# Graph attention's first fetch: attention columns as the weights, logits kept as rows in DRAM

## The reference

```
xl = (x @ W_l).reshape(n, H, C);  xr = (x @ W_r).reshape(n, H, C)
feat = xl[src] + xr[dst]
feat = jnp.where(feat >= 0, feat, NEG_SLOPE * feat)
logits = jnp.einsum('ehc,hc->eh', feat, att)
seg_max = jax.ops.segment_max(logits, dst, num_segments=n)
ex = jnp.exp(logits - seg_max[dst])
```

## Time and profile before

| | before |
|---|---|
| median of 3 runs, us | 10185.92 |
| profiled execution, us | 10172.71 |
| its span, us | 10170.6 |
| mean granted clock of TensorE, share of 2.4 GHz | 0.751 |
| PE / DVE / ACT / POOL busy, us | 5979.7 / 4870.8 / 2036.9 / 6515.4 |
| first fetch, 255 to 1640 us | 1385 |

### The profile page before, as it was taken

The page is one execution under the profiler, slowest core; times in us unless marked ns, Lnnn a source line. Parts: engine busy times, 40 slices in busy tenths (PEclk is TensorE's granted clock), DMA queues, the critical chain, the costliest instruction groups (busy, mean ns, idle before and its releaser), DMA issues. The chain is left out here.

```text
span 10170.6 us, 136884 instructions
## 1 busy us (share of the span) xinstructions
PE 5979.7 (59%) x24639; PEld 4757.3 (47%) x24640; DVE 4870.8 (48%) x14032; ACT 2036.9 (20%) x5514; POOL 6515.4 (64%) x9285
## 2 busy tenths in 40 slices
PE   4788885774666666645555344555455465455544
PEld 2677774553544444433334233444344344444443
DVE  6455556776644444445556333334333342455555
ACT  2111111783322222210000100001000031223324
POOL 3777772000058888888888688884888816777750
PEclk9788887997877777766667677777777765667767
DMA  4555555663067777764444333332333325677764
GB/s 151 169 173 178 171 176 195 200 199 108 2 105 105 105 105 104 105 112 135 140 139 130 120 89 90 88 90 80 89 89 89 90 83 158 223 231 241 249 201 158
DMA packets 863543, 1389.54 MB, mean 137 GB/s; under 512 B 114551, under 2 KB 516805, under 8 KB 862997
## 3 DMA queue, kind: packets, MB, share of 16 engines
q0 software_dynamic: 315328, 634.04, 27.7%
q1 hardware_dynamic: 366180, 501.57, 15.2%
q10 hardware_dynamic: 181488, 248.03, 7.3%
HBM read 955.84 MB, written 427.35 MB: 136 GB/s over the span
## 5 line engine op out<-in xcount | busy, mean ns | idle before, releaser
L1030 POOL DMA_INDIRECT regionB<-table,gather_rows x3136 | 3105.2, 990 | 1007.2 <-POOLq L1032 606.5
L1771 POOL DMA_INDIRECT scatter_sums<-regionC,idx x880 | 1388.3, 1578 | 306.2 <-issue 246.6
L1136 PE MATMUL ps_p<-regionB,hot 128*128 x3520 | 1039.8, 458 | 768.3 <-DVE regionC L1197 576.8
L1136 PEld LDWEIGHTS ps_p<-regionB,hot 128*128 128x128 f32 x3520 | 815.6, 235 | 977.1 <-issue 833.9
L1033 POOL MEMSET regionA<- 128x192 f32 x3920 | 1124.8, 287 | 5.8 <-remote 1.6
L1136 PE MATMUL ps_p<-regionC,hot 128*128 x1760 | 646.2, 511 | 554.4 <-issue 433.3
L1030 POOL DMA_INDIRECT regionC<-table,gather_rows x784 | 755.2, 963 | 156.6 <-issue 99.3
L2113 PE MATMUL ps_p<-regionA 128*128 128x264 f32 x1760 | 578.4, 497 | 417.9 <-PEq L2108 191.7
L1136 PEld LDWEIGHTS ps_p<-regionC,hot 128*128 128x128 f32 x1760 | 440.4, 257 | 760.1 <-issue 691.4
L1844 PE MATMUL psC<-regionC 128*128 128x128 f32 x1760 | 371.2, 377 | 647.0 <-PEq L1842 644.6
L1203 DVE TENSOR_TENSOR regionA<-ps_own,own_bias 128x256 f32<-128x256 f32 x98 | 41.6, 425 | 1371.0 <-DVEq L1202 1014.9
(11 more groups left out here) (366 smaller groups left out, 10280.1 us busy)
## 6 DMA issues: line engine op xcount, KB each, us to landing
regionA<-edge_rows SPq DMA_DIRECT2D x440, 256.0 KB, 3.3
regionA<-edge_rows ACTq DMA_DIRECT2D x440, 256.0 KB
edge_rows<-regionB SPq DMA_DIRECT2D x196, 512.0 KB
edge_rows<-regionB SPq DMA_DIRECT2D x392, 256.0 KB
regionC<-srcrow_d SPq DMA_DIRECT2D x220, 256.0 KB
scatter_sums<-zero_rows ACTq DMA_DIRECT2D x8, 6400.0 KB, 41.5
regionB<-table,gather_rows POOLq DMA_INDIRECT x3136
regionA<-scatter_sums ACTq DMA_DIRECT2D x49, 1024.0 KB
```

The source lines that it names most:

```text
L1030: g.indirect_dma_start(out=rows_of(b * per + j), out_offset=None, in_=table, in_offset=bass.IndirectOffsetOnAxis(ap=idx[:, column:column + ...
L1136: x = te.matmul(ps[(u.c * VG + j) % NB], hot[:, b, 2 * j + k, :], at_tile(G, slot[j] * 2 + k), start=k == 0, stop=k == 1)
L1771: g.indirect_dma_start(out=scat, out_offset=bass.IndirectOffsetOnAxis(ap=idx[:, b, j:j + 1], axis=0), in_=sums[:, b, j, :], in_offset=None ...
```

## The change

The roles in `logit` are exchanged: the attention columns (128x4) are the weights, and the transposed features of both steps of a visit (256 columns) are streamed against them, in two halves of the feature dimension. The result stands by head on 4 partitions. Two visits fill a PSUM bank; then ScalarE copies the 4x512 rows into SBUF and writes them by DMA to a new DRAM table `logits_by_step` of 880 x 4 x 128 (`logits_out`, now in ScalarE's list with a lag of 11). VectorE no longer copies logits, and the zeroing of `LG` goes. In the softmax SP loads that table, step on partitions, in seven transfers; the 28 transposes and seven masked copies become four multiplications in place. Before the last transfer, VectorE zeroes the last block of the target, and SP waits for that.

```diff
@@ -714,18 +715,24 @@
                                 if by_step:
                                     load(sp, valid, step_d.rearrange('p (c e) -> p c e', e=P))
                                     load(sp, etcol, et_d, allow_slow_non_contiguous=True)
+                                    for c in range(SB - 1):
+                                        load(sp, RS[:, :, c, :], logits_d[c * P:(c + 1) * P, :, :])
+                                    sp.wait_ge(aux_free[0], 1)
+                                    sp.sem_inc(aux_free[0], -1)
+                                    load(sp, RS[0:S - (SB - 1) * P, :, SB - 1, :], logits_d[(SB - 1) * P:S, :, :])
                                 loaded(sp)
                                 sp.sem_inc(aux_full[0], 1)
...
+                            if by_step:
+                                v.memset(RS[:, :, SB - 1, :], 0.0).then_inc(aux_free[0], 1)
...
-                                for c in range(SB):
-                                    b = c % 2
-                                    v.wait_ge(res_full[b], 1)
-                                    v.sem_inc(res_full[b], -1)
-                                    v.tensor_tensor(RS[:, :, c, :], ps[b][:, 0:512].rearrange('p (h e) -> p h e', e=P), valid[:, c, :].unsqueeze(1).to_broadcast([P, H, P]), ALU.mult).then_inc(own_v, 1)
-                                    v.wait_ge(own_v, 1)
-                                    v.sem_inc(own_v, -1)
-                                    v.sem_inc(res_free[b], 1)
+                                for h in range(H):
+                                    v.tensor_tensor(RS[:, h], RS[:, h], valid, ALU.mult)
...
-                        for t_ in turns(a, NV, 2 * VG, 9, written_out=True):
...
+                        def logits_out(u):
+                            q = u.val // 2
+                            b = q % 2
+                            if u.val % 2 == 0:
+                                return
+                            a.wait_ge(aux_full[b], 1)
+                            a.sem_inc(aux_full[b], -1)
+                            if q >= 2:
+                                a.wait_ge(s_load[b].sem, q // 2 * 16 + s_load[b].base)
+                            a.activation(rows_out[:, b, :], psL[b][0:HEADS0, :], ACT.Copy).then_inc(own_a, 1)
+                            a.wait_ge(own_a, 1)
+                            a.sem_inc(own_a, -1)
+                            a.sem_inc(aux_free[b], 1)
+                            a.dma_start(logits_d[4 * q:4 * q + 4, :, :].rearrange('s h e -> h s e'), rows_out[:, b, :].rearrange('h (s e) -> h s e', e=P)).then_inc(s_load[b].sem, 16)
+                        for b in (0, 1):
+                            a.sem_inc(aux_free[b], 1)
+                        for t_ in turns(a, NV, 2 * VG, 11, written_out=True):
...
+                            if t_.has(11):
+                                logits_out(t_.at(11))
+                        for b in (0, 1):
+                            a.wait_ge(aux_free[b], 1)
+                            a.sem_inc(aux_free[b], -1)
+                            a.wait_ge(s_load[b].sem, NV // 4 * 16 + s_load[b].base)
...
                         def logit(u):
-                            b, gb = (u.c % 2, u.c // VG % 2)
+                            b, gb = (u.c % 2, u.c // 2 % 2)
                             te.wait_ge(act_full[b], 1)
                             te.sem_inc(act_full[b], -1)
-                            if u.c % VG == 0:
+                            if u.c % 2 == 0:
                                 te.wait_ge(aux_free[gb], 1)
                                 te.sem_inc(aux_free[gb], -1)
-                            for k in (0, 1):
-                                col = (u.c % VG * 2 + k) * HEADS0
-                                for c in (0, 1):
-                                    x = te.matmul(psL[gb][:, col:col + HEADS0], featT[:, b, 2 * k + c, :], attc[:, c, :], start=c == 0, stop=c == 1)
-                            if u.c % VG == VG - 1:
+                            both = featT[:, b].rearrange('p (k c) n -> p c k n', c=2)
+                            for c in (0, 1):
+                                x = te.matmul(psL[gb][0:HEADS0, b * 2 * P:(b + 1) * 2 * P].rearrange('h (k n) -> h k n', k=2), attc[:, c, :], both[:, c], start=c == 0, stop=c == 1)
+                            if u.c % 2:
                                 x.then_inc(aux_full[gb], 1)
...
-                        v.memset(LG[:, :, :], 0.0).then_inc(own_v, 1)
-                        v.wait_ge(own_v, 1)
-                        v.sem_inc(own_v, -1)
-                        for b in (0, 1):
-                            v.sem_inc(aux_free[b], 1)
...
-                        def logits_out(u):
-                            gb = u.c // VG % 2
-                            if u.c % VG != VG - 1:
-                                return
-                            v.wait_ge(aux_full[gb], 1)
-                            v.sem_inc(aux_full[gb], -1)
-                            v.tensor_copy(LG[:, bass.ds((u.val - (VG - 1)) * 2, GS), :], psL[gb][:, 0:GS * HEADS0].rearrange('p (s h) -> p s h', h=HEADS0)).then_inc(aux_free[gb], 1)
-                        for t_ in turns(v, NV, 2 * VG, 7, written_out=True):
+                        for t_ in turns(v, NV, 2 * VG, 3, written_out=True):
```

More of the change, by code:

```diff
@@ L140, in build @@
         wgt_d = dram('weights_by_step', [P, S])
+        logits_d = dram('logits_by_step', [S, HEADS0, P])
         srccol_d = dram('sources_by_step', [P, S])
@@ L721, in _ @@
                         def _(te):
-                            for c in range(SB):
-                                b = c % 2
[L724 to L728, removed]
+                            if not by_step:
+                                for c in range(SB):
+                                    b = c % 2
+                                    te.wait_ge(res_free[b], 1)
+                                    te.sem_inc(res_free[b], -1)
+                                    for h in range(H):
+                                        x = te.transpose(ps[b][:, h * P:(h + 1) * P], mine[:, c * P:(c + 1) * P, h], ident[:, :])
+                                    x.then_inc(res_full[b], 1)
                             if by_step:
@@ L1259, in attention_fetch0 @@
             spread = part(room, RG0 * EG * D + GS * P, [2, GS * P])
+            rows_out = part(room, RG0 * EG * D + 3 * GS * P, [2, 4 * P])[0:HEADS0]
             s_rows = plain_rows
@@ L1434, in attention_fetch0 @@
             s_used.base += NV
+            for b in (0, 1):
+                s_load[b].base += 16 * (NV // 4)
             for b in range(RG0):
```

4 lines of the change are left out of this document (removed).

## The result

The changed kernel took 10123.8 us (median of 5 runs, 10104.6 to 10144.0), the kernel before 10183.4 us on the same chip (10169.6 to 10193.1): a ratio of 0.9943, 95% interval 0.9926 to 0.996. That is 60 us faster. The forecast of 10065 us lies 118 us under the kernel before; the direction and the wide range (9955 to 10210) held, the size and the forecast's own range (10025 to 10115) did not.

The account below looks back on a forecast made before the run. TensorE sets the fetch's pace while its clock is low, POOL's gathers would at high clock. Fetch -133, stage end +4, softmax +14 make -115 us against 10172.7, giving 10058; with the runs' higher median, 10065 was said, range 9955 to 10210.

Parts of the forecast that it names:

- The clock: First fetch, TensorE: clock returns within about one visit after a stall; a third of 471 us remains, saving 153 us.
- The first rival: First fetch, TensorE after a stall: four-column logits do not lift the clock; about 10215 us, chance 0.20.
- the price of a visit at full clock: First fetch, TensorE: 0.05 us more on each of 400 visits at 2.4 GHz, costing 20 us; visit 2.19 us.
- The third rival: First fetch: stalls spread as faster TensorE leaves POOL fewer pauses; half the saving given back, about 10140 us, chance 0.13.
- eight instructions fewer a visit: First fetch: argument against spreading stalls, that eight of 32 instructions go from each visit.
- The logits on TensorE: First fetch: four 256-column records at the fetch's price, +0.05 us a visit at 2.4 GHz, +0.15 at 1.2 GHz.
- my bound of +0.15: First fetch, TensorE logits: upper bound on the direct cost per visit in us; the lower bound was -0.41.
- POOL as the bound: First fetch: rival that POOL's gathers bound throughout; its 173 us of waiting included, 193 us go, about 10010 us, chance 0.17.
- The seam: Start of softmax: logit loads +17 us, multiplications replacing masked copies -3, together +14 us.
- my upper bound: Start of softmax: +30 us, if loads in 512-byte pieces run at half speed.
- The end of the stage: End of first fetch: waits for a DMA instead of a VectorE copy of 0.18 us, +4 us.
- ScalarE and VectorE in the fetch: First fetch: VectorE's dropped logit copies (20 us) worth nothing; ScalarE's added 205 us of copies and DMA issues cost nothing.

Follow-up runs that it names:

- e9: The kernel before, unaltered, traced on chip 8; its fetch ended at 1630.1 us.
- e10: The changed kernel, unaltered, traced on chip 8; its fetch ended at 1573.9 us.
- e13: Changed kernel with attention columns zero-padded to 128 and zero rows held behind the logits' loads, chip 3; 0.9932 of the kernel before.
- e14: Changed kernel with attention columns zero-padded to 128, chip 3, all gathers; its fetch ended at 1580.5 us.
- e15: Same kernel as e14, run again on chip 3 for the spread between executions; its fetch ended at 1576.4 us.
- e2: Kernel before with each fetch matmul issued twice (1760 more 256-column records), chip 15; 10055.9 us, 1.0078 of the kernel before.
- e16: Changed kernel with columns padded to 128 and every second node-row gather of the first fetch left out, chip 3; fetch ended at 1240.0 us.
- e12: Changed kernel (4 columns) with every second node-row gather of the first fetch left out, chip 8; fetch ended at 1336.8 us.
- e7: Changed kernel with columns padded to 128 and POOL's memset behind each gather of this fetch 288 columns instead of 192; fetch ended at 1529.8 us.
- e8: As e7, but with a memset of 64 columns; 1.0112 of the kernel before, fetch ended at 1646.5 us.
- e4: Changed kernel with ScalarE's zero rows held until SP's softmax loads landed, chip 15; first VectorE work 11.7 us after first load, not 22.9.
- e1: Changed kernel with attention columns zero-padded to 128, chip 15; 0.9959 of the kernel before, fetch ended at 1512.3 us.

## Why the prediction was right, and where it failed

*The clock: right in its sum, in part by luck.* A third of the 471 us at 1.2 GHz should remain, 157; measured are 2 x (1 - 0.95) x 1319 = 132. But the reason given was a clock that comes back within about one visit of a stall. It comes back after 7.5 us in the mean, three visits, against 11.1 before; the rest comes of falls that went from 42 to 18 (37 to 19 in e9 and e10), on which the forecast does not count. ScalarE's copies over 1 us late went from 187 to 200 (those over 3 us from 92 to 75), so it is not that the stalls are gone. The first rival, a clock at or under 0.83, is refuted by the 0.95. The Trainium skill (TensorE: Matmul & The Clock Gate, HAM oscillation) has waits put the clock down and the next burst start slow. The stretches at 470 and 385 agree; that the falls would then remain as many, as the prediction read it, the 42 and 18 refute.

*The step that failed* is the price of a visit at full clock: "With 0.05 us more on the 400 visits then at 2.4 GHz (20 us)". From the records of the last 431 visits: before, 292 at full clock took 722 us (2.47 each), the other 139 took 605. After, 398 at full clock took 1086 us (2.73), the other 33 took 175. (Where a visit is cut moves these counts by a few.) The 106 visits that changed sides had held 430 us and at 2.47 us take 262, which saves 168 where 153 were forecast; 0.26 us more on 398 visits cost 103 where 20 were forecast. That leaves 65, and the stage saved 66. The same sum over e9 and e10 has 115 in place of 168 and 74 in place of 103.

That is a sum and not yet a cause, and a second step failed behind it: the prediction adds up visits as if each term stood by itself. e13, e14 and e15 bring the visit back to 2.17 us, and their fetch ends no sooner in the mean. Their visits at full clock take 2.54 to 2.61 us in the mean, but 44 to 51 visits are not at full clock and hold 265 to 300 us. What the shorter visit gives goes back to stalls and to the low clock; why it is so nearly all of it stays open.

The third rival, spreading stalls with half of the saving given back, has 10140 us, nearer than my 10065, but by luck: ScalarE's copy is 1.66 us late in the mean before and 1.57 after, over 3 us in 92 visits and in 75, so the stalls did not spread. That eight instructions fewer a visit spoke against it is not tested by a run that changes this number alone; e2, with eight records more a visit, has fewer late copies (94). In the sum itself, 10058 and the 13 us of the median make 10071, not the 10065 that I wrote.

*The logits on TensorE: mis-sized.* The +0.05 us a visit was the fetch's price; +0.27 came, outside my bound of +0.15, through the width of the weights. The Trainium skill (same page, Part 2, Step-by-step: what each phase is for) says that a weight load can be pulled ahead while matmuls run. The rows at 1565.12 agree for 128 columns behind 128; at 1566.19, behind a change of width, they do not. The rule of the Trainium skill that I weighed (same page, Part 3), that a narrow matmul takes as long as a full one, was kind: it took longer, 0.96 us against 0.86. Without stalls the change of width is worth 97 us (e16 and e12), with all gathers nothing that the traces on chip 3 show, and 8 to 20 us on chip 15.

*POOL as the bound: not reached.* By the prediction's own sum (784 x (1.022 + 0.285 + 0.16) + 24.3 = 1174 us, between 263.1 and 1529.5) POOL still waits 92 us where it waited 173. It becomes the bound by way of more pause (e7), at nearly the same end. In e7 and e8 the stage lies between two limits that meet: gather faster and the stalls grow, slower and the gathers last longer.

*The seam: right in kind.* +14 forecast, +10.5 measured; the loads share with the zero rows (e4), and no run shows the half speed of 512-byte pieces that stood behind my upper bound. The end of the stage, +4 forecast, +4.9 measured. *ScalarE and VectorE in the fetch:* at nothing, as the idle time of ScalarE (960 us) suggests; no run takes their work away alone.

*Open:* why results of TensorE are taken over late while POOL gathers. ScalarE is not what is late: of the 92 copies of the kernel before that are over 3 us late, 89 begin within 0.3 us behind the semaphore event that tells of the transposes, and that event comes 5.3 us in the mean behind their modelled end. Nor do loads of program text account for it all: in 52 of the 92 no packet of the instruction queues starts between 3 us ahead of that end and the copy. Open, too: what differs between the chips, since no trace of the kernel before came from chip 15; whether a pause between 192 and 288 columns is better.

## What to carry to other kernels

A low clock is a symptom with a cause ahead of it: what lifts the clock wins only what the cause leaves. Price a new instruction by a row with the same neighbours on its engine: the fetch's 0.86 us stood between weights of one width, the logits do not. Do not add up savings on one engine as if its waits stayed as they are: 0.24 us less a visit gave nothing in e13 to e15. Before a saving on one engine is believed, take the suspected neighbour's work away by half; those runs showed more than any sum. And weights that alternate on TensorE are cheaper with one width, though that paid in full only where nothing stalled.

## What was not expected of the hardware

- A change of the weights' width, 128 to 4 or 64 and back, costs 0.24 to 0.29 us a visit: the load waits for the matmul before it (2.41 and 2.46 us against 2.17).
- Indirect gathers on POOL at 1.39 us and more apart go with results of TensorE that are handed on late: ScalarE's copy starts 1.57 us behind the transposes in the mean, and over 3 us in 62 visits (e1). At 1.47 us and more it is 0.57 us and 4 visits (e7). In the kernel before it is TensorE's semaphore that comes late, behind ends that are modelled. Nothing in the profile shows what the two share.
- Seven DMA issues on SP took 12.49 us while ScalarE's queue wrote zero rows, 5.54 us without them (11.1 to 12.5 and 5.5 to 6.0 in the other traces).
- With weights of 4 columns and 256 streamed ones in place of eight loads of 128, TensorE's granted clock fell 18 times in the fetch instead of 42, with as many late copies.
